# Layer 0 of a four-layer graph network on one core: edge weights held in a PSUM bank of their own, the chain's two small banks merged into one

## The reference, cut to what matters

```python
h = jnp.einsum('nf,fhd->nhd', x, W)
a_src = jnp.sum(h * att_src, axis=-1)
a_dst = jnp.sum(h * att_dst, axis=-1)
e = jax.nn.leaky_relu(a_src[src] + a_dst[dst], NEG_SLOPE)
e_max = jax.ops.segment_max(e, dst, num_segments=N)
e_exp = jnp.exp(e - e_max[dst])
denom = jax.ops.segment_sum(e_exp, dst, num_segments=N)
out = jax.ops.segment_sum(h[src] * (e_exp / (denom[dst] + 1e-16))[:, :, None], dst, num_segments=N)
x = _layernorm(x + relu(out + bias))
```

## Time and profile before

| | us |
|---|---|
| median of three runs | 5281.45 |
| lowest and highest run | 5277.9, 5286.8 |
| the profiled execution, its own time | 5284.91 |
| its span | 5283.1 |
| outside the span | 1.8 |
| layer 0's loop, first to last step (start of the first L1354 to the end of the last adds) | 138 to 1209 |

### The profile page before, as it was taken

How to read it: one execution, slowest core, us unless ns; L and a number is a source line. 1 busy time by engine, 2 the same in 40 slices (tenths; PEclk the granted TensorE clock), 3 DMA queues, 4 the chain that set the end, 5 groups by cost and what they waited for, 6 DMA issues and landing times.

```text
span 5283.1 us, 86663 instructions
## 1 busy us (share of the span) xinstructions
PE 3888.6 (74%) x13357; PEld 2393.2 (45%) x13357; DVE 3504.2 (66%) x10780; ACT 2567.7 (49%) x6941; POOL 3861.1 (73%) x3995
## 2 busy tenths in 40 slices
PE   7888888886777777677777777676777657666663
PEld 5666666663444444344434434343334334444442
DVE  5889888885555455354444445666666578888887
ACT  3667666674555555355555551000000166666665
POOL 3777777766777777677777776777777777777775
PEclk8889889898998999777787787878887777777776
DMA  6444444433333333443333333333333322222222
GB/s 171 117 123 123 123 122 122 124 108 106 110 112 111 112 111 112 127 133 112 113 112 111 112 112 100 109 109 109 109 110 109 97 57 57 57 57 57 57 57 67
DMA packets 252627, 549.14 MB, mean 104 GB/s; under 512 B 71467, under 2 KB 136235, under 8 KB 252108
## 3 DMA queue, kind: packets, MB, share of 16 engines
q0 software_dynamic: 178752, 478.34, 33.3%
q1 hardware_dynamic: 45804, 42.37, 2.6%
q10 hardware_dynamic: 27552, 22.89, 1.5%
HBM read 501.16 MB, written 42.15 MB: 103 GB/s over the span
## 4 chain that ended last, share of the span: by engine, by line
POOL 55%; issue 20%; PE 10%; ACT 6%; DVE 4%; DMA 2%; SPq 1%; DVEq 0%; ACTq 0%; POOLq 0%
POOL scratch L1416 41%; POOL scratch L1886 14%; PE bank L1312 5%; PE bank L1161 3%; ACT scratch L1073 2%; DMA scratch<-tab_x,src_idx 1%; DVE reg_acc L1337 1%; PE bank L1149 1%; ACT scratch L1085 1%; DVE reg_x L1354 1%; SPq L872 1%; ACT scratch L1076 1%; DMA scratch<-tab_h,src_idx 1%; POOL reg_x L1031 0%; ACT scratch L1121 0%
## 5 line engine op out<-in xcount | busy, mean ns | idle before, releaser
L1468 PE MATMUL bank<-scratch 128*128 x4986 | 1904.2, 495 | 761.6 <-SPq L1428 407.3
L1478 DVE TENSOR_TENSOR reg_acc<-reg_acc,bank 128x256 f32 x2493 | 1048.1, 420 | 1361.7 <-PE bank L1468 1298.4
L1416 POOL DMA_INDIRECT scratch<-tab_x,src_idx x1566 | 1491.5, 952 | 533.3 <-issue 469.4
L1468 PEld LDWEIGHTS bank<-scratch 128*128 128x128 f32 x4986 | 964.3, 228 | 1602.9 <-issue 1549.0
L1031 POOL DMA_INDIRECT reg_x<-tab_h,src_idx x832 | 831.6, 1000 | 291.0 <-issue 176.7
L1416 POOL DMA_INDIRECT scratch<-tab_h,src_idx x783 | 744.4, 951 | 260.7 <-issue 234.3
L1886 POOL DMA_INDIRECT scratch<-tab_h,src_idx x783 | 741.2, 947 | 248.6 <-issue 237.7
L1937 PE MATMUL bank<-reg_w,scratch 128*128 128x260 f32 x1664 | 637.5, 527 | 286.6 <-issue 185.2
L1437 ACT ACTIVATE scratch<-iota_row,dst_loc 128x128 f32<-128x128 f32 x1662 | 572.1, 392 | 348.2 <-PE bank L1468 333.9
L1312 PE MATMUL bank<-reg_x,scratch 128*128 128x265 f32 x1664 | 577.8, 458 | 73.3 <-DVE reg_x L1354 71.1
L1937 PEld LDWEIGHTS bank<-reg_w,scratch 128*128 128x128 f32 x1664 | 377.3, 253 | 509.7 <-issue 312.1
(11 more groups left out here) (314 smaller groups left out, 4374.9 us busy)
## 6 DMA issues: line engine op xcount, KB each, us to landing
scratch<-tab_x,src_idx POOLq DMA_INDIRECT x1566, 2.8
scratch<-tab_h,src_idx POOLq DMA_INDIRECT x1566, 2.7
reg_x<-tab_h,src_idx POOLq DMA_INDIRECT x832
tab_h<-scratch ACTq DMA_DIRECT2D x7, 924.0 KB, 6.4
reg_x<-in_x SPq DMA_DIRECT2D x7, 896.0 KB, 11.3
reg_w<-in_x SPq DMA_DIRECT2D x49, 128.0 KB, 2.5
tab_x<-reg_acc SPq DMA_DIRECT2D x49, 128.0 KB
tab_xs<-reg_w SPq DMA_DIRECT2D x49, 128.0 KB, 2.7
```

Source lines behind the costliest of these rows:

```text
L1416: e.indirect_dma_start(ring_rows[:, j % SLOTS, :], None, self.table, bass.IndirectOffsetOnAxis(ap=src_idx[:, j:j + 1], axis=0)).then_inc(* ...
L1468: e.matmul(self.bank(i), ring_hots[:, i % HOTS, :], rows, start=True, stop=True).then_inc(*self.product.up)
L1478: e.tensor_tensor(v, v, self.bank(i), ALU.add).then_inc(*self.added.up)
```

## The change

- psum[7] becomes weights0, two halves (for even and odd groups) of 128 columns: 16 steps by 8 heads. ACT still writes the weights into the rows; a new DVE copy, move_weights, takes them from there to weights0 once per group, after the last piece of step 15 of the group before. The copy waits for ACT's weights. The multiplies wait for the copy (s_moved) and read their weights from PSUM.
- bank_c moves into psum[6], which also holds bank_3 and bank_d. The turned larger goes to columns 0 to 127.
- begins moves on PE from k = 7, ahead of dst_scores(2), to k = 8, behind dst_scores(3); begin_col on ACT from k = 8 to k = 9. DVE's node (L1248) gets a wait for ACT's part.
- The third one-hots (hot 2) come at k = 3, ahead of step_masks, instead of at k = 4.

```diff
+        weights0 = psum[7][:, 0:2 * S * H].rearrange("p (g s h) -> p g s h", g=2, h=H)
...
-        bank_t, bank_3, bank_d, bank_c = (psum[4], psum[5]), psum[6][:, 0:3 * P], psum[6][:, 3 * P:4 * P], psum[7]
+        bank_t, bank_3, bank_d, bank_c = (psum[4], psum[5]), psum[6][:, 0:3 * P], psum[6][:, 3 * P:4 * P], psum[6]
...
-                if k in (0, 2, 4, 5):
-                    hot((0, 2, 4, 5).index(k))
+                if k in (0, 2, 3, 5):
+                    hot((0, 2, 3, 5).index(k))
...
-                if k == 8:
+                if k == 9:
                     e.wait_ge(*ch_t.at("begins", g))
                     e.copy(begin_col, bank_c[:, 256:258]).then_inc(*ch_a.done("begin_col"))
...
-                    e.transpose(bank_c[:, 3 * P:4 * P], second[:, 0:P], ident[:, :]).then_inc(*ch_t.done("larger"))
+                    e.transpose(bank_c[:, 0:P], second[:, 0:P], ident[:, :]).then_inc(*ch_t.done("larger"))
...
             if k == 7:
+                dst_scores(2)
+            if k == 8:
+                dst_scores(3)
                 e.wait_ge(*ch_a.at("begins", g))
                 e.wait_ge(*h0_v.at("begins"))
                 for n in range(2):
...
-                dst_scores(2)
-            if k == 8:
-                dst_scores(3)
...
                 v = rank_value(e, "vector", g * S)
+                e.wait_ge(*ch_a.at("part", g))
                 e.tensor_tensor(node_both.rearrange("p (k h) -> p k h", k=2),
...
+            def move_weights(g):
+                e.wait_ge(*ch_a.at("weights", g))
+                if g >= 2:
+                    e.wait_ge(*weighted0((g - 1) * S - 1))
+                e.tensor_copy(weights0[:, g % 2], group0(g)[0][:, :, FEAT:ROW0]).then_inc(*moved0.up)
...
-                row = rows0[:, i % (3 * S), :]
-                v = row[:, 0:FEAT].rearrange("p (h d) -> p h d", h=H)
-                e.wait_ge(*ch_a.at("weights", g))
-                e.tensor_tensor(v, v, bcast(row[:, FEAT:ROW0], 2, [P, H, D]), ALU.mult).then_inc(*weighted0.up)
+                v = rows0[:, i % (3 * S), 0:FEAT].rearrange("p (h d) -> p h d", h=H)
+                e.wait_ge(*moved0(g))
+                e.tensor_tensor(v, v, bcast(weights0[:, g % 2, k, :], 2, [P, H, D]), ALU.mult).then_inc(*weighted0.up)
...
+                if k == S - 1 and g + 1 < GROUPS:
+                    move_weights(g + 1)
```

More of the change, by code:

```diff
@@ L347, in build @@
         s_chain = {n: signal(f"{n}_chain") for n in ("vector", "tensor", "scalar")}
+        s_moved = signal("weights_moved")
         s_far, s_hot4 = signal("distance_made"), signal("four_hots_made")
@@ L905, in build @@
         level = small[0:1, 400:400 + 4 * H].rearrange("p (k f) -> p k f", k=2)
-        bank_t, bank_3, bank_d, bank_c = (psum[4], psum[5]), psum[6][:, 0:3 * P], psum[6][:, 3 * P:4 * P], psum[7]
+        bank_t, bank_3, bank_d, bank_c = (psum[4], psum[5]), psum[6][:, 0:3 * P], psum[6][:, 3 * P:4 * P], psum[6]
         h0_a = a_order.named("middle_clear start_clear end_clear")
+        moved0 = s_moved.take(GROUPS)
         h0_v = v_order.named("level begins ones src_less src_below src_at")
@@ L1006, in build @@
         ch_t = s_chain["tensor"].named(
-            "turned3 hots0 hots1 dst0 tails hots2 dst1 hots3 begins dst2 dst3 larger", GROUPS)
+            "turned3 hots0 hots1 dst0 tails hots2 dst1 hots3 dst2 dst3 begins larger", GROUPS)
         ch_a = s_chain["scalar"].named(
-            "upright hot0 kept3 hot1 kept_hot0 step_masks hot2 kept_tails kept_hot1 hot3 begins kept_hot2 kept_hot3 "
+            "upright hot0 kept3 hot1 kept_hot0 hot2 step_masks kept_tails kept_hot1 hot3 begins kept_hot2 kept_hot3 "
             "begin_col part shrink weights", GROUPS)
@@ L1264, in chain_vector @@
                 e.wait_ge(*ch_t.at("larger", g))
-                e.tensor_tensor(both[:, P:2 * P], bank_c[:, 3 * P:4 * P], dst_part,
+                e.tensor_tensor(both[:, P:2 * P], bank_c[:, 0:P], dst_part,
                                 ALU.add).then_inc(*ch_v.done("larger_added"))
@@ L1344, in heads_vector @@
             e.tensor_tensor(src_at_i, src_at, src_below, ALU.add).then_inc(*h0_v.done("src_at"))
+            def move_weights(g):
[3 more added lines that the diff above has]
+                e.tensor_copy(weights0[:, g % 2], group0(g)[0][:, :, FEAT:ROW0]).then_inc(*moved0.up)
             for k in range(S):
                 chain_vector(e, 0, k)
+            move_weights(0)
             e.wait_ge(*pre_p.at("rest_clear"))
```

## The result

The changed kernel takes 5394.48 us, median of 5 runs (5392.37 to 5407.06), against 5281.45: a ratio of 1.0219, with a 95% interval of 1.0208 to 1.0231. That is 113 us more, where 69 were forecast; the direction was right, and the time lies 4 us over the upper end of the whole range (5290 to 5390). The profiled execution took 5407.06 us, the longest of the five, so its rows show some 13 us more than the median.

What follows compares the result with a forecast made beforehand. The bound was taken as a ring through three engines, with ACT and DVE waiting on each other, and POOL in a few groups. 68 + 4 + 0 + 8 + 0 + 2 - 13 = 69 us; forecast 5350 us, range 5290 to 5390.

Steps and rivals of the forecast that it cites:

- begins behind the target scores: On PE, begins after dst_scores(3) delays begin_col and stops DVE about 105 us; 68 us left after later waits.
- The wait of node for part: DVE's node waiting for ACT's part: covered by the two scans, except for closings at step 9; 4 us.
- move_weights: DVE's copy of weights to PSUM, once a group: 8 us (bounds 0 and 15), the kept-tails wait taking back most.
- The multiply from PSUM: DVE's multiplies reading weights from PSUM: no difference taken; 11 us the upper end, 54 us by the skill's fixed cost.
- POOL: POOL's gathers get faster, under 975 ns; only DVE's landing waits are on the path: -13 us (ends 0 and -13).
- the rival in which POOL sets the pace: POOL's gathers set the loop's pace, so faster gathers make the kernel faster: 5241 to 5255 us; chance 0.09.
- The third one-hots and the prologue: ACT's hot(2) changing places with step_masks: nothing; the scan starting later in the prologue: 2 us (ends 1 and 3.5).
- The ring had no play: Rival that the ring has play: DVE's later waits swallow its stop, 5281 to 5290 us; chance 0.09.
- the rival's time of 5395: PE's clock in the loop falls to 0.80: 34 us, with 11 for the multiply, makes 5395; chance 0.10.

Runs made afterwards that it cites:

- begins early: Changed kernel with begins turned and read in the one-hots' bank psum[4], ahead of dst_scores(2), begin_col again at step 8: 5291.53 us, ratio 1.0021.
- the kernel with the late copy: Against the kernel with begins early: copy behind step 6's multiply, for steps 7 to 15 only; steps 0 to 6 multiply from the rows: 5277.31 us, ratio 0.9984.

## Why the prediction was right in direction and short in size

**begins behind the target scores.** Right in mechanism and near in size. Stop of DVE: forecast 105 us, measured 111.8 more. Per group at full clock 1.7 us were worked out, and the 34 such groups had 1.65; those of a low clock had up to 4.9. What later waits give back was set at 37 (68 left of 105), and the products and the turned larger gave back 31.9. So this term was 80, not 68.

**The wait of node for part.** The cover held: 2.4 us, in 4 groups. But the step asked only what the semaphore costs. It left out what DVE's sequencer does at that place, the load of 16 tile numbers, which older work had hidden. This is the term that the sum did not have at all: 17.6 us more of idle time. Moving the whole load off, with the 6.8 us that it had shown before, gave back 30 us of run time. It comes with the stop and not with the wait for part, since the kernel with the order alone has it too, 22.0 us in all.

**move_weights.** Half of it was thought to be swallowed by the wait for the kept tails. The sign for this, a wait that shrinks by up to 15 us, failed: it grew by 8.4 us. Most of that is the order's, since with the order alone it grew by 7.5; with the copy taken out of the changed kernel it is 59.1 in place of 62.9, so the copy did not shorten it. The copy was paid in full, 14 to 16 us for the 8 of the forecast.

**The multiply from PSUM.** Right: 410 ns after and 414 before. The 65 ns more that the page's fixed cost of the PSUM source would have given (the Trainium skill, VectorE: DVE Perf Modes, "The TRN2 errata — SBUF-src ops pay a fixed extra latency per instruction") do not appear; the measurement decides. The weights are one of two operands here, and the features stay in SBUF.

**POOL.** Right: gathers fell to 959 ns, POOL now waits for PE 225.1 us with stops of up to 3.5, and landing waits are gone. With both operands in SBUF they stayed at 991, so it is the second SBUF operand of the multiply that stretched them, as the Trainium skill has it (SBUF — State Buffer, "Who interferes with whom"). In the changed kernel it was worth nothing that can be seen, as the forecast said against the rival in which POOL sets the pace. The 13 us of landing waits went, as forecast, but they went with the order alone too, so the order accounts for them and the gathers need not. With begins early a small gain is not excluded: the kernel with the late copy, whose gathers are faster and whose landing wait is 3.2 us in place of 29.0, lies 0.2% below the one that multiplies from the rows throughout, with intervals (0.9973 to 0.9996, 0.9996 to 1.0013) that just meet.

**The third one-hots and the prologue.** Nothing, as said, for the first. The prologue took 3.8 us where 2 were said, with an upper end of 3.5; the first copy, 0.3 us, stands in it.

**The rivals.** The ring had no play: a delay of half the size passed on after its slack. The clock did fall, from 0.89 to 0.83, not to 0.80, and the rival's time of 5395 is the one measured; that agreement is luck, since 11 us of it were for a slower multiply that did not come and 34 for a deeper fall of the clock. The sum over DVE's own rows comes out without a separate term for the clock, but a part of the stop is the clock's. An estimate from the counts above: at the stops measured for each kind of group (1.65, 4.0 and 2.2 us), the 40, 4 and 7 groups of the kernel before would have stopped DVE for 97 us, so some 16 of the 113.6 come from more groups standing at the low clock. How much of the run time that is, no run separated. With begins early the clock is back at 0.90.

Put together, from the profiled execution: 80 for the stop, 17.6 for the load, 16 for the copy, 8.4 for the kept tails, 2.4 for part, 1.8 for the first scans' wait and 4 for the prologue, less 13 for landing, is 117, as much as loop and prologue grew there; the forecast had 69. The 48 us between them are 17.6 of the load, 12 of the stop, 8.4 of the kept tails, 8 of the copy and 2 of the rest. The step that failed is the costing of what stands behind a new stop in program order and round the ring: the load on DVE's sequencer was put at nothing and measured 17.6 us, the copy was put at 8 and measured 14 to 16, and the wait for kept tails was to take time back and grew by 8.4. The term for the stop itself was right in kind and 12 us short.

## What to carry to other kernels

When an edit makes an engine stop where it used to run through, its sequencer stops as well: list the register loads and other issue work behind the new stop, because they come out of hiding, and here half a microsecond in 48 of 51 groups made as much as the copy. Look at the order that comes with a shared bank before the bank itself: here the order cost the time and the merged bank nothing that can be seen, and the same bank was freed at no cost by turning the result into another bank that was idle at that moment. (No run kept the old order in the merged bank, so whether that bank needs the new order is not shown.) Try a small copy just ahead of a wait that its engine has anyway, not in front of the first use of a new group: here that was 14 us better, though the late copy was also a little smaller, and seven steps of a group did not need it.

## What the runs showed of the hardware

The multiply with one operand in SBUF and one in PSUM takes as long as with both in SBUF (410 and 414 ns for 256 columns), and the indirect gathers beside it go from 1000 to 959 ns, or from 991 with the copy made and not used. A load of 16 registers on DVE shows as 0.48 us of issue when nothing queued covers it, and the gap is gone when the load stands ahead of the stop. The granted clock of the loop went mostly with DVE's stops: 0.89 in the kernel before and 0.90 with begins early; 0.83 in the changed kernel, which stopped DVE for 114 us; 0.85 with the order alone and in the changed kernel with the load moved, which stopped it for 105 and 113. But it also stood at 0.87 in the kernel before with the load moved, which has no such stop, so the stops are not all that moves it.
